# First attention: mixing weights multiplied into the queries, the two decay scales summed before one head sum

## The chip, the cores and the metric

The kernel runs on one core of one Trainium2 chip. The time is the device time of one execution in microseconds (us). The engines are TensorE (PE; PEld is its weight load), VectorE (DVE), ScalarE (ACT), GpSimd (POOL) and SyncE (SP), which issues the DMAs.

## What is computed

Four blocks are added to a residual x of 16 sequences, 256 tokens and 128 channels: the first attention (a), a dense eight-expert feed-forward, a second attention (b), and the feed-forward again. Only the first attention changes. It has 32 heads of 4 channels and two decay scales m. The mixing weight mt is a softmax over the two scales.

```python
phi_q = elu(rope(x @ Wq.T)) + 1            # phi_k likewise
def step(carry, xs):                       # over the tokens
    S, K = carry
    pq, pk, vt, bt, mt = xs
    K = K * bt[..., None] + pk[:, :, None, :]
    S = S * bt[..., None, None] + pk[:, :, None, :, None] * vt[:, :, None, None, :]
    num = einsum('bhd,bhmdc->bhmc', pq, S)
    den = einsum('bhd,bhmd->bhm', pq, K) + EPS
    y = sum(num / den[..., None] * mt[..., None], axis=2)
x = x + layernorm_affine(ln(x) + y @ Wout.T + bout)
```

## The kernel before, in words

The 4096 tokens are cut into 8 tiles of 512 (two sequences). A program loop runs over t = -1 to 9 and, inside, over 32 chunks c (8 experts times 4 slices of 128 hidden units). In step (t, c) each engine's stream first issues its share of the feed-forward of tile t - 2 (`ffn_pe`, `ffn_act`, `ffn_dve`, `ffn_pool`) and then what its own `attn(t, c)` puts at that chunk. So tiles 0 and 1 of the attention run without a feed-forward beside them, tiles 2 to 7 run beside the feed-forward of tiles 0 to 5, and the feed-forward of tiles 6 and 7 has no first attention beside it. The streams are in order; the chunk numbers are an order written out by hand, and semaphores hold what depends.

Feed-forward of a chunk: PE makes `gate` (3 matmuls of 512 columns, split in high and low parts, L338 to L340), `up` (3) and `down` of the chunk three back (3). ACT makes the SiLU (L537) and the high part of the hidden tile (L547). DVE multiplies (L577). The low part (L553) is made by DVE for even chunks and by POOL for odd ones, one chunk later. PE's `up` of a chunk waits for DVE's product of the chunk two back, and `down` waits for the low part. While tile 2 runs, ACT (L461) and POOL (L466) also split the weights of the eight experts.

First attention of a tile, `[128 = 4 channels x 32 heads, 512 tokens]` a piece: PE projects k, q (each twice for the rotation), the two decay rates b0, b1, the mixing logits (mx) and four value pieces v0 to v3 (`project`). DVE makes phi (L1511, c = 10), four products KV = phi_k * v (L1524) and ten scans (L1534): for each scale four numerator components (m, 0) to (m, 3) and one denominator (m, 4). The scanned states are multiplied by phi_q: scale 0 on DVE (L1541: one of 512 and two of 1024), scale 1 on POOL (`product`, L743, five of 512). PE sums over channels with 0/1 matrices in float32: `numerator` (L1107, four per scale, 512 columns), `denominators` (L1117, four of 256 columns) and, once DVE has made weights WGT = (1 + tanh) / den (L1609, L1611, L1616), `weights` (L1128, spreads them to the channels). In the trace each float32 matmul shows as two records. ACT copies the spread weights to RS (L927), DVE multiplies them with the two numerators (`weighted`, L1518), POOL adds the scales to Y (L768), and `project_y` (L1135, L1139) projects Y at chunk 0 of the next tile. The DVE line L1550 takes that result; everything of the next norm and of the residual of this tile follows from it.

## Time and profile before

| | us |
|---|---|
| median of 3 runs | 1755.48 |
| lowest, highest | 1751.98, 1756.20 |
| the profiled execution: its own time | 1751.74 |
| its span | 1749.9 |
| busy: PE | 1625.6 (93%) |
| busy: DVE | 1071.4 (61%) |
| busy: ACT | 1014.7 (58%) |
| busy: POOL | 886.4 (51%) |

The span runs from the first to the last instruction; what is said of durations below is from that one profiled execution. PE records overlap, since a matmul is loaded while the one before it drains: the time that one takes is the distance between starts, not its own duration. The first attention lies in the first 670 us; the second attention lies around 790 to 1170 us, and feed-forwards fill the rest.

### The profile page before, as it was taken

The page shows a single profiled execution, that of the slowest core. Times are in us where ns is not written, and L with a number is a line of the kernel's source. Part 1 is how long each engine was busy: PE and PEld are TensorE (multiplying, and loading weights), DVE is VectorE, ACT ScalarE, POOL GpSimd, SP SyncE. Part 2 cuts the span into 40 slices and gives each one's busy share as a digit, 9 for nine tenths or more (in the row PEclk, how much of TensorE's full clock was granted, in tenths as well). Part 3 has the DMA queues.
Part 4 walks back from the last instruction along what each step waited for, and adds up shares of the span by engine and source line. Part 5 has one row for each costly group of instructions (what it writes and reads, how often), then busy time and mean ns, then how long its engine had stood idle before and what let it go on. Part 6 is the DMA issues. An engine that isn't in the chain of part 4 may idle for free. (4 is left out here: it accounts for less than half of the span.)

```text
span 1749.9 us, 24769 instructions
## 1 busy us (share of the span) xinstructions
PE 1625.6 (93%) x7232; PEld 1253.1 (72%) x7232; DVE 1071.4 (61%) x1871; ACT 1014.7 (58%) x1871; POOL 886.4 (51%) x793
## 2 busy tenths in 40 slices
PE   3588999999999999995899999997999999999998
PEld 2356777777777878883566666665888888888887
DVE  5667777777778685452676676652554555554544
ACT  2236474747464646552577787785555555555554
POOL 3668664646464544333477777784333332333332
PEclk9888999999999999995999999998999999999999
DMA  4035444444443435640000000002555556555553
GB/s 122 1 110 197 151 146 143 145 145 145 141 146 135 145 136 189 212 157 0 1 1 2 2 1 0 1 16 81 181 192 204 194 182 207 193 188 195 195 199 133
DMA packets 72548, 215.88 MB, mean 123 GB/s; under 512 B 7387, under 2 KB 20832, under 8 KB 72416
## 3 DMA queue, kind: packets, MB, share of 16 engines
q1 hardware_dynamic: 72416, 214.35, 35.7%
q8 instruction: 55, 0.90, 0.2%
q14 instruction: 77, 0.63, 0.1%
HBM read 199.64 MB, written 14.68 MB: 122 GB/s over the span
## 5 line engine op out<-in xcount | busy, mean ns | idle before, releaser
L553 POOL TENSOR_TENSOR ARENA_R<-ARENA,ARENA_R 128x512 fp32r<-128x512 f32 x256 | 344.3, 1345 | 605.6 <-ACT ARENA_R L547 604.9
L577 DVE TENSOR_TENSOR ARENA<-ARENA,pair 128x512 f32<-128x512 f32 x512 | 349.2, 682 | 453.7 <-PE pair L340 417.2
L537 ACT ACTIVATE ARENA<-bank 128x512 f32<-128x512 f32 x512 | 306.3, 598 | 471.5 <-PE bank L340 470.5
L338 PE MATMUL pair<-ARENA_R 128*128 128x512 f32 x1064 | 416.9, 392 | 18.6 <-POOL ARENA_R L553 8.3
L340 PE MATMUL pair<-ARENA_R 128*128 128x512 f32 x1064 | 415.0, 390 | 0.0
L339 PE MATMUL pair<-ARENA_R 128*128 128x512 f32 x1064 | 414.3, 389 | 0.0
L547 ACT ACTIVATE ARENA_R<-ARENA 128x512 fp32r<-128x512 f32 x512 | 319.6, 624 | 32.8 <-DVE ARENA L577 30.9
L871 POOL TENSOR_TENSOR ARENA_R<-ARENA,ARENA_R 128x512 fp32r<-128x512 f32 x192 | 249.4, 1314 | 79.9 <-ACT ARENA L1048 76.3
L338 PE MATMUL bank<-ARENA_R 128*128 128x512 f32 x568 | 239.7, 422 | 23.3 <-DVE ARENA L1524 18.1
L338 PEld LDWEIGHTS pair<-ARENA_R 128*128 128x128 f32 x1064 | 200.8, 189 | 67.9 <-POOL ARENA_R L553 10.0
L340 PEld LDWEIGHTS pair<-ARENA_R 128*128 128x128 f32 x1064 | 200.9, 189 | 42.3
L339 PEld LDWEIGHTS pair<-ARENA_R 128*128 128x128 f32 x1064 | 201.1, 189 | 41.2
L339 PE MATMUL bank<-ARENA_R 128*128 128x512 f32 x568 | 223.5, 393 | 0.0
L340 PE MATMUL bank<-ARENA_R 128*128 128x512 f32 x568 | 223.4, 393 | 0.0
L553 DVE TENSOR_TENSOR ARENA_R<-ARENA,ARENA_R 128x512 fp32r<-128x512 f32 x256 | 195.0, 762 | 0.1
L1648 DVE TENSOR_REDUCE ARENA<-bank 128x2 f32<-128x512 f32 (+1 forms) x192 | 131.0, 689 | 86.5 <-PE bank L1257 56.4
L338 PEld LDWEIGHTS bank<-ARENA_R 128*128 128x128 f32 x568 | 108.2, 190 | 52.4 <-DVE ARENA L1524 21.8
L1293 PE MATMUL pair<-ARENA_R 128*128 128x512 f32 x384 | 135.2, 433 | 8.5 <-ACT ARENA L1028 6.9
L1048 ACT ACTIVATE ARENA_R<-pair 128x512 fp32r<-128x512 f32 x192 | 115.6, 602 | 34.4 <-PE pair L1281 26.0
L339 PEld LDWEIGHTS bank<-ARENA_R 128*128 128x128 f32 x568 | 108.4, 191 | 23.5 <-issue 4.3
L340 PEld LDWEIGHTS bank<-ARENA_R 128*128 128x128 f32 x568 | 107.9, 190 | 23.3
L1534 DVE TENSOR_TENSOR_SCAN ARENA<-ARENA 128x512 f32<-128x512 f32 x80 | 121.5, 1526 | 0.0
(213 smaller groups left out, 2037.7 us busy)
## 6 DMA issues: line engine op xcount, KB each, us to landing
ARENA_R<-split_weights SPq DMA_DIRECT2D x360, 512.0 KB, 4.8
split_weights<-ARENA_R SPq DMA_DIRECT2D x24, 512.0 KB, 3.8
X<-in_L_attn_a_x_dram SPq DMA_DIRECT2D x8, 256.0 KB, 5.5
ARENA<-in_L_ffn_Wg_dram SPq DMA_DIRECT2D x8, 256.0 KB, 2.9
ARENA<-in_L_ffn_Wu_dram SPq DMA_DIRECT2D x8, 256.0 KB, 3.2
ARENA<-in_L_ffn_Wd_dram SPq DMA_DIRECT2D x8, 256.0 KB, 3.8
out_dram<-X SPq DMA_DIRECT2D x8, 256.0 KB, 4.3
CST<-in_tables_dram SPq DMA_DIRECT2D x1, 835.5 KB, 4.5
```

The source lines that it names most:

```text
L338: pe.matmul(dst, wh, xh, start=start, stop=False)
L339: pe.matmul(dst, wh, xl, start=False, stop=False)
L340: return pe.matmul(dst, wl, xh, start=False, stop=stop)
L537: act.activation(SG[:, c % 2, :], bank[c % 2], ACT.Silu).then_inc(F.sil, 1)
L547: act.activation(HH[:, G % FC, :], HF[:, G % FC, :], ACT.Copy).then_inc(F.hh, 1)
L553: eng.tensor_tensor(HL[:, G % FC, :], HF[:, G % FC, :], HH[:, G % FC, :].bitcast(F32), ALU.subtract).then_inc(lo_done(G)[0], 1)
L577: v.tensor_tensor(HF[:, c % FC, :], SG[:, c % 2, :], bank[2 + c % 2], ALU.mult).then_inc(F.mul, 1)
L871: g.tensor_tensor(PL[:, u % RING, :], PT[:, u % RING, :], PH[:, u % RING, :].bitcast(F32), ALU.subtract).then_inc(B.pl, 1)
L1048: act.activation(dst[:, u % RING, :], bank[2 + u % 2], ACT.Exp, scale=DB ** -0.5).then_inc(B.t_used, 1)
L1293: m = pe.matmul(bank[4 + qb], VS[:, p, 2 * ob + kb, at:at + P], (PH, PL)[i][:, u % RING, :], start=(u < 2 and i == 0), stop=(g == NG - 1 a ...
L1534: v.tensor_tensor_scan(S[:, m, c, :], BETA[:, m, :], KV[:, c, :], 0.0, ALU.mult, ALU.add).then_inc(A.scan, 1)
L1648: v.tensor_reduce(dst, src, AX.X, ALU.max, negate=True).then_inc(B.row_used, 1)
```

## The change

`PQM[m]` = phi_q times the spread weight of scale m is made on DVE (`weighted`, two of 512, reading PSUM directly). The numerator states are then multiplied by PQM instead of phi_q, scale 0 on DVE (`product`, two of 1024) and scale 1 on POOL (four of 512). POOL adds the two scales component by component (`sum_scales`, four of 512), PE makes one head sum of four float32 matmuls in place of two, and ACT copies it to Y. The two denominator products are both POOL's (`product_z`). ACT's two copies to RS, DVE's 512 product and POOL's addition to Y are gone. The order of the scans, the denominators, the weights and the head sum over the chunks changes with it; `SCANS` lists the new order of the scans for the waits.

```diff
+SCANS = [(0, 4), (1, 4), (0, 0), (0, 1), (1, 0), (0, 2), (0, 3), (1, 1), (1, 2), (1, 3)]
...
+        def scanned(t, m, c):
+            return A.scan, 10 * t + SCANS.index((m, c)) + 1
...
@@ gpsimd
-            def product(t, i):
-                c = (4, 0, 1, 2, 3)[i]
-                g.wait_ge(A.scan, 10 * t + 5 + i + 1)
-                g.wait_ge(A.phi_q, t + 1)
-                g.tensor_tensor(S[:, 1, c, :], S[:, 1, c, :], PQ[:, :], ALU.mult).then_inc(A.prod1, 1)
+            def product_z(t, m):
+                g.wait_ge(*scanned(t, m, 4))
+                g.wait_ge(A.phi_q, t + 1)
+                g.tensor_tensor(S[:, m, 4, :], S[:, m, 4, :], PQ[:, :], ALU.mult).then_inc(A.prodz, 1)
+            def product(t, c):
+                g.wait_ge(*scanned(t, 1, c))
+                g.wait_ge(A.pq, 2 * t + 2)
+                g.tensor_tensor(S[:, 1, c, :], S[:, 1, c, :], PQM[:, 1, :], ALU.mult).then_inc(A.prod1, 1)
+            def sum_scales(t, c):
+                g.wait_ge(A.prod0, 2 * t + c // 2 + 1)
+                g.wait_ge(A.prod1, 4 * t + c + 1)
+                g.tensor_tensor(S[:, 0, c, :], S[:, 0, c, :], S[:, 1, c, :], ALU.add).then_inc(A.sum, 1)
...
-                    if c in (19, 21, 22, 23, 24):
-                        product(t, (19, 21, 22, 23, 24).index(c))
-                    if c == 30:
-                        g.wait_ge(A.ay, 2 * (t + 1))
-                        after(g, A.z, t)
-                        g.tensor_tensor(Y[:, :], RS[:, 0, :], RS[:, 1, :], ALU.add).then_inc(A.y, 1)
+                    if c in (13, 14):
+                        product_z(t, c - 13)
+                    if c in (20, 24, 26, 27):
+                        product(t, (20, 24, 26, 27).index(c))
+                    if c in (23, 25, 27, 28):
+                        sum_scales(t, (23, 25, 27, 28).index(c))
...
@@ scalar
-                    if c == 27:
-                        weight_rows(t, 0)
-                    if c == 28:
-                        weight_rows(t, 1)
+                    if c == CH - 1:
+                        act.wait_ge(A.num, t + 1)
+                        after(act, A.z, t)
+                        act.activation(Y[:, :], bank[7], ACT.Copy).then_inc(A.y, 1)
...
@@ tensor
+                if is_tile(t) and c == 15:
+                    pe.wait_ge(a_used["v2"], t + 1)
+                    denominators(t)
...
-                    if c == 20:
-                        pe.wait_ge(a_used["v3"], t + 1)
-                        numerator(t, 0, (0, 1))
-                    if c == 22:
-                        numerator(t, 0, (2, 3))
-                        pe.wait_ge(a_used["v2"], t + 1)
-                        denominators(t)
-                    if c == 24:
-                        pe.wait_ge(n_a.lo, min(t + 2, NT))
-                        after(pe, n_f.lo, t)
-                        numerator(t, 1, (0, 1))
-                    if c == 25:
-                        numerator(t, 1, (2, 3))
-                    if c == 26:
+                    if c == 18:
                         weights(t, 0)
+                        weights(t, 1)
                     if c == 27:
-                        weights(t, 1)
+                        pe.wait_ge(A.pq, 2 * (t + 1))
+                        numerator(t, (0, 1))
+                    if c == 30:
+                        numerator(t, (2, 3))
...
@@ vector
+                v.wait_ge(A.rep, 2 * t + m + 1)
+                v.wait_ge(A.phi_q, t + 1)
...
+                v.tensor_tensor(PQM[:, m, :], PQ[:, :], bank[(5, 7)[m]], ALU.mult).then_inc(A.pq, 1)
```

DVE's `attn(t, c)` now reads, chunk by chunk: 11 KV 0, scan (0,4); 12 scan (1,4); 13 KV 1 and 2; 14 scan (0,0); 15 KV 3; 16 denominator plus epsilon and reciprocal; 17 WGT, scan (0,1); 18 scan (1,0); 19 `weighted` 0 and 1; 20 scan (0,2); 21 scan (0,3); 22 `product` of components 0 and 1; 23 scan (1,1); 24 `product` of 2 and 3; 25 scan (1,2); 26 scan (1,3). Before, the last scan stood at 23, the reciprocal at 24, WGT at 25 and `weighted` at 28 and 29. Below, L numbers of rows of the kernel before are its own; the changed kernel's are a few lines further on.

DVE in tile 0, from the first KV product, before (L1524 KV, L1534 scan, L1541 product):

```order
L1524 TENSOR_TENSOR ARENA<-ARENA,bank 128x512 x2
L1534 SCALAR_TENSOR_TENSOR ARENA<-ARENA 128x512
L1524 TENSOR_TENSOR ARENA<-ARENA,pair 128x512
L1534 SCALAR_TENSOR_TENSOR ARENA<-ARENA 128x512
L1524 TENSOR_TENSOR ARENA<-ARENA,bank 128x512
L1534 SCALAR_TENSOR_TENSOR ARENA<-ARENA 128x512 x3
L1541 TENSOR_TENSOR ARENA<-ARENA 128x512
L1541 TENSOR_TENSOR ARENA<-ARENA 128x1024
L1534 SCALAR_TENSOR_TENSOR ARENA<-ARENA 128x512
L1541 TENSOR_TENSOR ARENA<-ARENA 128x1024
```

And changed (L1528 KV, L1538 scan, L1594 and L1596 the reciprocal, L1601 WGT, L1522 `weighted`):

```order
L1528 TENSOR_TENSOR ARENA<-ARENA,bank 128x512
L1538 SCALAR_TENSOR_TENSOR ARENA<-ARENA 128x512 x2
L1528 TENSOR_TENSOR ARENA<-ARENA,bank 128x512
L1528 TENSOR_TENSOR ARENA<-ARENA,pair 128x512
L1538 SCALAR_TENSOR_TENSOR ARENA<-ARENA 128x512
L1528 TENSOR_TENSOR ARENA<-ARENA,bank 128x512
L1594 TENSOR_SCALAR ARENA<-pair 128x256
L1596 RECIPROCAL ARENA<-ARENA 128x256
L1601 SCALAR_TENSOR_TENSOR ARENA<-ARENA 128x256
L1538 SCALAR_TENSOR_TENSOR ARENA<-ARENA 128x512 x2
L1522 TENSOR_TENSOR ARENA<-ARENA,pair 128x512
L1522 TENSOR_TENSOR ARENA<-ARENA,bank 128x512
```

The reciprocal has moved from behind all ten scans to behind three of them.

POOL in tile 0, from the first norm's small operations to the end of the tile, before (L743 product, L768 the sum to Y):

```order
L363 TENSOR_SCALAR VE<-MV 128x4
L364 TENSOR_SCALAR NM<-MV 128x4
L366 TENSOR_TENSOR RSTD<-VE,HALF 128x4
L368 TENSOR_TENSOR NB<-NM,RSTD 128x4
L743 TENSOR_TENSOR ARENA<-ARENA 128x512 x5
L768 TENSOR_TENSOR ARENA<-ARENA 128x512
```

And changed (L747 `product_z`, L753 `product`, L759 `sum_scales`):

```order
L371 TENSOR_TENSOR RSTD<-VE,HALF 128x4
L373 TENSOR_TENSOR NB<-NM,RSTD 128x4
L747 TENSOR_TENSOR ARENA<-ARENA 128x512 x2
L753 TENSOR_TENSOR ARENA<-ARENA 128x512
L759 TENSOR_TENSOR ARENA<-ARENA 128x512
L753 TENSOR_TENSOR ARENA<-ARENA 128x512
L759 TENSOR_TENSOR ARENA<-ARENA 128x512
L753 TENSOR_TENSOR ARENA<-ARENA 128x512 x2
L759 TENSOR_TENSOR ARENA<-ARENA 128x512 x2
```

Six large operations have become ten.

## Rows read from the trace of the kernel before

**Rows 1.** The span in 40 equal slices, busy tenths.

```profile
PE   3588999999999999995899999997999999999998
DVE  5667777777778685452676676652554555554544
```

**Rows 2.** Busy time by stretch: tile 0, tile 1, tile 2, tile 4.

```profile
core 0: us, PE busy (x) PEld busy (x) DVE busy (x) ACT busy (x) POOL busy (x), PEclk, DMA share, GB/s
32.10:61.80 29.70, 14.74 (x40) 7.22 (x40) 24.67 (x25) 3.90 (x8) 13.40 (x8) 0.83 0.00 1
78.70:109.10 30.40, 17.12 (x43) 8.57 (x43) 25.38 (x28) 7.55 (x16) 17.40 (x15) 0.72 0.00 1
112.00:212.00 100.00, 91.15 (x364) 69.35 (x363) 75.07 (x103) 58.25 (x109) 80.82 (x63) 0.94 0.53 184
...
420.60:464.40 43.80, 42.07 (x174) 31.49 (x173) 43.54 (x50) 22.35 (x43) 24.12 (x21) 1.00 0.42 142
```

**Rows 3.** Order of time, PE, tile 4 (start, us, line, count), two numerator matmuls.

```profile
443.67 0.39 PE L340 MATMUL pair<-ARENA_R 128*128 128x512 f32 x1
443.90 1.88 PE L1107 MATMUL bank<-ARENA,CST 128*128 128x512 f32 x4
...
445.84 0.40 PE L339 MATMUL bank<-ARENA_R 128*128 128x512 f32 x1
```

**Rows 4.** Order of time, PE, where projection of Y begins, tiles 4 and 5.

```profile
390.72 0.39 PE L1135 MATMUL bank<-BBA,ONESR 128*128 128x512 f32 x1
...
477.48 0.39 PE L338 MATMUL bank<-ARENA_R 128*128 128x512 f32 x1
...
479.52 0.39 PE L1135 MATMUL bank<-BBA,ONESR 128*128 128x512 f32 x1
```

**Rows 5.** Order of time, DVE, tile 4, chunks 10 to 26.

```profile
420.64 0.65 DVE L577 TENSOR_TENSOR ARENA<-ARENA,pair 128x512 f32<-128x512 f32 x1
...
426.15 1.21 DVE L1534 TENSOR_TENSOR_SCAN ARENA<-ARENA 128x512 f32<-128x512 f32 x1
...
449.80 1.40 DVE L553 TENSOR_TENSOR ARENA_R<-ARENA,ARENA_R 128x512 fp32r<-128x512 f32 x1
451.12 2.28 DVE L1534 TENSOR_TENSOR_SCAN ARENA<-ARENA 128x512 f32<-128x512 f32 x1
...
464.44 0.69 DVE L577 TENSOR_TENSOR ARENA<-ARENA,pair 128x512 f32<-128x512 f32 x1 [0.27 <-PE pair L340]
```

**Rows 6.** Order of time, POOL, tile 4.

```profile
449.37 1.28 POOL L743 TENSOR_TENSOR ARENA<-ARENA 128x512 f32<-128x512 f32 x1 [2.89 <-DVE ARENA L1534]
450.61 1.71 POOL L553 TENSOR_TENSOR ARENA_R<-ARENA,ARENA_R 128x512 fp32r<-128x512 f32 x1
```

**Rows 7.** Order of time, DVE, tile 0.

```profile
32.08 1.29 DVE L1511 SCALAR_TENSOR_TENSOR ARENA<-ARENA 128x512 f32<-128x512 f32 x2 [3.62 <-ACT ARENA L916]
...
49.11 3.79 DVE L1534 TENSOR_TENSOR_SCAN ARENA<-ARENA 128x512 f32<-128x512 f32 x2
...
53.24 1.75 DVE L1611 RECIPROCAL ARENA<-ARENA 128x256 f32<-128x256 f32 x1
```

**Rows 8.** Order of time, POOL, tiles 0 and 1.

```profile
44.29 10.89 POOL L743 TENSOR_TENSOR ARENA<-ARENA 128x512 f32<-128x512 f32 x5 [10.86 <-DVE ARENA L1534]
...
84.90 0.80 POOL L368 TENSOR_TENSOR NB<-NM,RSTD 128x4 f32<-128x4 f32 x1
```

**Rows 9.** Order of time, PE, tiles 0 and 1.

```profile
48.23 1.89 PE L1117 MATMUL pair<-ARENA,CST 128*128 128x256 f32 x8
...
61.79 0.51 PE L1135 MATMUL bank<-BBA,ONESR 128*128 128x512 f32 x1 [2.75 <-POOL ARENA L768]
...
109.14 0.77 PE L338 MATMUL bank<-ARENA_R 128*128 128x512 f32 x1 [2.65 <-POOL ARENA_R L466]
```

**Rows 10.** Order of time, DVE, tiles 1 and 2.

```profile
78.69 1.26 DVE L1511 SCALAR_TENSOR_TENSOR ARENA<-ARENA 128x512 f32<-128x512 f32 x2
...
145.01 2.90 DVE L1511 SCALAR_TENSOR_TENSOR ARENA<-ARENA 128x512 f32<-128x512 f32 x2
```

More of the change, by code:

```diff
@@ L252, in program @@
         WGT = take(SEQ)
-        RS = take(MA, TOK)
+        PQM = take(MA, TOK)
         Y = take(TOK)
@@ L922, in half_tanh @@
                                scale=0.5).then_inc(a_used[f"b{m}"], 1)
-            def weight_rows(t, m):
-                act.wait_ge(A.rep, 2 * t + m + 1)
-                after(act, A.y, t)
-                act.activation(RS[:, m, :], bank[5], ACT.Copy).then_inc(A.rs, 1)
             def attn(t, c):
@@ L1125, in weights @@
                 else:
[L1126 removed]
+                    pe.wait_ge(a_used["v3"], t + 1)
                 for b in range(SPT):
[L1128 removed]
+                    x = pe.matmul(bank[(5, 7)[m]][:, b * SEQ:(b + 1) * SEQ], cst(f"rep_{2 * b + m}"), WGT[:, :],
                                   start=True, stop=True)
@@ L1529, in scan @@
                     v.wait_ge(a_used[f"v{c}"], t + 1)
-                    after(v, (A.num0, A.num1)[m], t)
+                    after(v, A.num, t)
                 else:
@@ L1602, in attn @@
                     if c == 22:
+                        product(t, 0, 2)
+                    if c == 23:
+                        scan(t, 1, 1)
+                    if c == 24:
+                        product(t, 2, 4)
+                    if c == 25:
                         scan(t, 1, 2)
-                    if c == 23:
+                    if c == 26:
                         scan(t, 1, 3)
-                    if c == 24:
-                        v.wait_ge(A.den, t + 1)
-                        after(v, A.wgt, t)
-                        v.tensor_scalar(RC[:, :], bank[5][:, 0:SEQ], DEN_EPS, None, ALU.add).then_inc(A.dp, 1)
-                        v.wait_ge(A.dp, t + 1)
-                        v.reciprocal(RC[:, :], RC[:, :]).then_inc(A.rc, 1)
-                    if c == 25:
-                        v.wait_ge(A.rc, t + 1)
-                        v.wait_ge(a_used["mx"], t + 1)
-                        after(v, A.rep, 2 * t)
-                        v.scalar_tensor_tensor(WGT[:, :], MIX[:, :], 1.0, RC[:, :], ALU.add,
-                                               ALU.mult).then_inc(A.wgt, 1)
-                    if c == 28:
-                        weighted(t, 0)
-                    if c == 29:
-                        weighted(t, 1)
             for t in range(-1, NT + 2):
```

73 lines of the change are left out of this document (39 added, 34 removed).

## The prediction, made before the changed kernel ran

> **What bounds the kernel now.** I read the busy tenths first [rows 1]: PE stands at 9 from the fifth slice on, but for two short dips, and at 3 to 8 in the first four (to 175 us); DVE stands at 7 or 8 from the fourth to the thirteenth slice, and at 5 or less in the last third. So I took the busy time by stretch [rows 2]. Three kinds of stretch come out. Tiles 0 and 1 (no feed-forward beside them): PE is busy 14.7 of 29.7 us and DVE 24.7, with gaps; a chain of waits, not an engine, sets the time. Tile 2: PE 91, DVE 75 and POOL 81 of 100 us, since POOL also splits weights. Tile 4, which stands for tiles 3 to 7: over chunks 10 to 25 (43.8 us) PE is busy 42.1 us and DVE 43.5. Both are full there; elsewhere in the tile DVE is not. After tile 7 the change touches nothing.
>
> Next the order of time in those stretches. In tile 4 DVE runs without a gap from 420.64 us (product of chunk 10) and first waits for PE again at 464.44, chunk 26 [rows 5]. So in those chunks PE does not wait for DVE only because its own head sums give DVE time: they lie in chunks 20 to 26.
>
> Two DVE figures recur. A scan alone takes 1.21 us, 1.14 from start to start, and a low part 0.68 (0.60). Beside POOL they take 2.28 and 1.40 [rows 5]: POOL's L743 runs from 449.37 and its L553 from 450.61 to 452.32 [rows 6], and the DVE operations with two operands in SBUF end about one operation after POOL's does. In tile 0 it works both ways: five POOL products that take 1.28 each alone fill 10.89 us [rows 8]. The products that read PSUM keep their 0.65 to 0.69. I therefore count DVE's two-SBUF-operand work and POOL's large operations as taking turns.
>
> The Trainium skill (SBUF — State Buffer, Who interferes with whom) has it that a DVE instruction with two SBUF inputs and a GpSimd instruction that reads SBUF exclude each other for a whole instruction; by that rule the trace agrees on single pairs. On average a POOL operation has cost DVE less than a whole one here, as worked out below.
>
> **The change, part by part.** Eight tiles change.
>
> PE. The group of two float32 matmuls starts at 443.90 and the regular pace (0.227 between starts) resumes at 445.84 [rows 3], so it takes 445.84 - 0.227 - 443.90 = 1.71 us, 0.85 each. Four fewer: -3.4 us a tile. Denominators and weights stay, at other places.
>
> ACT: one copy instead of two, -0.6 us, off the path. DVE: minus a 512 product, 0.6 us. POOL: ten large operations instead of six, +5.2 us a tile.
>
> *Tiles 3 to 7.* DVE from chunk 10 through 26, start to start and without POOL: 17 products 10.0, 8 low parts 4.8, two phi 1.2, four KV 2.4, ten scans 11.4, two 1024 products 2.4, two subtractions 1.2, epsilon and reciprocal 2.1, WGT 0.5, and now both `weighted` too, 1.2: 37.2 us. The same list for the kernel before, through chunk 25, is 36.1, and took 43.8 [rows 5]: 7.7 too much, 0.75 of it in the phi, 6.9 through 13 large POOL operations (eight low parts, five products), 0.53 each. Now there are 15 in the stretch (two `product_z` come in at chunks 13 and 14): 8.0. Then one new wait. `denominators` stands at PE's chunk 15 and needs `product_z` 1, which in POOL's queue lies behind the norm's small operations and a low part. By my walk it ends at 434.1, while PE arrives at 432.5: PE stalls about 1.7 us, and DVE, whose chunk 16 multiplies `up` of that chunk, idles 1.4. Sum 37.2 + 0.75 + 8.0 + 1.4 = 47.4, so the last scan ends at 420.6 + 47.4 = 468.0.
>
> Behind it POOL still has to do `product` 3, `sum_scales` 2, the low part of 27 and `sum_scales` 3: with one clash 5.6 us, to 473.6. PE's chunk 30 waits for it: last head-sum matmul and latency to 474.8, then chunk 31 (9 matmuls, 2.04) to 476.9. In the kernel before, chunk 31 ends at 477.48, two us ahead of the projection at 479.52 [rows 4]. That is -0.6 us a tile instead of -3.4. The period is 479.52 - 390.72 = 88.80 us before [rows 4]; I expect 88.2. The ends: PE hidden by nothing, -3.4; every extra POOL operation at its full 1.3 instead of 0.53, +1.5. Five tiles: **-3 us** (-17 to +7).
>
> *Tile 0.* Before, phi starts at 32.08 [rows 7] and the projection at 61.79 [rows 9]. I walk the new order from 32.08. KV 0 ends at 33.9, scan (0,4) at 35.0, scan (1,4) at 36.2. `product_z` 0 then has its turn to 37.4, scan (0,0) to 38.5, `product_z` 1 to 39.7. PE has had nothing since its transposes, and the granted clock averages 0.83 in this stretch [rows 2]; four 256-column float32 matmuls took 1.89 warm [rows 9], I take 3.0: 42.8. DVE, with nothing left since 39.1, waits 3.7 us. Epsilon and reciprocal (53.24, 1.75) [rows 7]: 45.1. WGT 45.5, two scans 47.8, two `weighted` 49.0. From there DVE's scans and products and POOL's products and sums take turns nearly one to one, as they did from 44.29 on before [rows 8]: `product` 0 of POOL 51.3, scan (0,3) 52.4, subtraction and 1024 product 54.1, scan 55.3, sum 56.4, 1024 product 57.5, POOL product 58.7, scan 59.8, sum 61.0, scan 62.1, and then POOL alone with product 2, product 3, sum 2, sum 3: 67.2. Head sum 68.4, copy 69.1, projection 69.2. Against 61.79: **+7 us** (+4 to +10). The tail behind the last scan is shorter than before (the last scan ended at 52.9 [rows 7], 8.9 us before the projection; now 7.1), but the last scan comes ten us later: reciprocal, WGT and `weighted` now stand ahead of it, 3.8, the denominator wait is 3.7, and the clashes are about 3.
>
> *Tile 1.* From phi at 78.69 [rows 10] to the first feed-forward matmul at 109.14 [rows 9] was 30.45 us. The walk is the same, 35.1 from phi to the last sum, plus about 2 because POOL's two sets of small norm operations run until 85.7 [rows 8], seven us after phi, and `product_z` stands behind them; then one weight part on POOL, 1.3: 38.4. **+8 us** (+4 to +11).
>
> *Tile 2.* POOL is busy 81 of 100 us [rows 2], DVE's chunk 10 begins its phi at 145.01 with 2.90 instead of 1.29 for the pair [rows 10]. DVE and POOL saturate each other, `product_z` waits behind weight parts (I find 4 us at PE's chunk 15), and 4 large operations come in, 5.2 us, while PE's 3.4 us are no gain where PE waits. Nearest rows: +5.2 if all of it lies on the path, 0 if PE's saving pays it. **+5 us** (0 to +9).
>
> Sum: 7 + 8 + 5 - 3 = +17 us. The profiled execution took 1751.74, so 1768.7; it lies 3.7 under the median of the three runs, and on the median 1755.48 the sum is **1772.5 us**.
>
> **The rivals.** (1) *PE's saving survives.* If DVE's chunks drain faster than I count (fewer clashes, no wait at chunk 15), tiles 2 to 7 get 3.4 each, -20; with the lower ends of tiles 0 and 1, +8, and 0 to +6 for what PE's stall in tile 2 leaves, the total is -12 to -6: about 1748. For it: PE is busy 42.1 of 43.8 us, so every us taken from it is room. Against it: DVE is busy 43.5 of the same. It decides if DVE can finish chunk 26 before about 465.5. This is the case on the other side of no change.
>
> (2) *A wash.* The prologue costs its lower ends, +8, tile 2 +2 and the steady tiles -1.5 each: +2.5, 1758. For it: a walk always lets two things collide that miss each other on the chip.
>
> (3) *The port, not the queue, decides.* If each added POOL operation holds DVE for its whole length, tiles 3 to 7 cost +1.5 instead of -0.6: +10 more, 1783. For it: single pairs behave so [rows 5, 6]. Against it: the average of 0.53 in the same stretch. This is what the exclusive lock that the Trainium skill states (SBUF — State Buffer, summary table) would make of it if the added operations always came first.
>
> (4) *The change does not do what it says*: PE keeps all its matmuls, or the order is the old one. The orders above exclude it; no chance.
>
> **How the numbers follow.** Forecast (+10 to +24 us) 0.58; rival 3 0.14; rival 2 0.16; rival 1 0.12. 0.3% is 5.3 us, about what a measurement of this kernel can tell from no change. Faster by more: most of rival 1, 0.10. Within: rival 2 and a little of the first, 0.17. Slower: 0.73. The range leaves out most of rival 1 below and the last of rival 3 above: 1756 to 1786.
>
> **What would show it.** PE has 64 fewer float32 records of the head sum (64 instead of 128, 0.85 us a matmul). Projection of tile 0 at about 69 us instead of 61.8, with a DVE gap of 2 to 4 us ahead of the epsilon line, and ten us more from phi to the last scan. In tile 1, about 38 us from phi to the first feed-forward matmul. Period of tiles 3 to 7 near 88.2 us, with PE gaps ahead of the denominators (released by POOL's `product_z`) and of the second half of the head sum (released by `sum_scales`), which were none before, and DVE without a gap from chunk 17 to 26. I would be wrong if the period fell to 86 us or less (PE's saving survives), or if the first projection came before 64 us.

## The result, and the profile after

| | kernel before | changed kernel |
|---|---|---|
| median (lowest to highest) | 1754.64 us (1751.98 to 1756.2), 4 runs | 1772.96 us (1772.31 to 1773.14), 4 runs |
| own time of the profiled execution | 1751.74 us | 1772.87 us |
| its span, mean granted clock | 1749.9 us, 0.969 | 1771.1 us, 0.960 |

The changed kernel takes 1.0105 times the time of the one before, 95% interval 1.0088 to 1.0123: slower by 18.3 us between medians. The forecast was 1772.5. The profiled execution of before lies 3 us under its median, that of the changed kernel on its own; between the two profiled executions, and so in everything read from traces below, the difference is 21 us.

To place it, I use milestones that both traces have: the start of the phi operations in tiles 0 and 1, and DVE's first read of the output projection in each tile (the reader, a few us behind the matmul that the prediction calls the projection of Y).

| us | before | changed | difference | forecast |
|---|---|---|---|---|
| start of phi, tile 0 | 32.08 | 32.61 | +0.5 | 0 |
| phi to reader, tile 0 | 31.14 | 39.66 | +8.5 | +7 |
| reader to phi of tile 1 | 15.47 | 16.38 | +0.9 | 0 |
| phi to reader, tile 1 | 39.03 | 45.58 | +6.6 | +8 |
| reader to reader, tile 1 to 2 | 100.00 | 105.18 | +5.2 | +5 |
| four periods to tile 6, each | 88.80 | 88.85 | +0.2 in all | -0.6 each |
| period to tile 7 | 88.13 | 87.69 | -0.4 | -0.6 |
| reader of tile 7 | 661.04 | 682.51 | +21.5 | +17 |

Behind the last reader both kernels take 1089 us. The loss lies before the reader of tile 2, which comes after 218 us in the kernel before and after 239 us in the changed one.

The page of the changed kernel shows it in its slices. The first line is busy time (share of the span) and instructions by engine, then come busy tenths of the span in 40 slices of 44.3 us, and the granted clock in tenths:

```profile
PE 1612.2 (91%) x7168; PEld 1240.4 (70%) x7168; DVE 1083.5 (61%) x1863; ACT 1010.0 (57%) x1863; POOL 937.6 (53%) x825
...
PE   4458799999999999996799999997999999999998
...
DVE  4567859696969596453566666762555554554544
...
PEclk9659999999999999997799999998999999999999
```

PE stood at 8, 8 and 9 in the third to fifth slices before [rows 1]; now it reads 5, 8 and 7. The granted clock is at 6 and 5 tenths in the second and third slices. The busy time by stretch, for tile 0 (phi to projection), tile 1 (phi to the first feed-forward matmul) and tile 4 (product of chunk 10 to the last scan), answers to [rows 2]:

```profile
core 0: us, PE busy (x) PEld busy (x) DVE busy (x) ACT busy (x) POOL busy (x), PEclk, DMA share, GB/s
32.60:69.70 37.10, 16.06 (x31) 7.76 (x31) 26.75 (x24) 3.34 (x7) 18.76 (x12) 0.60 0.00 0
88.60:127.00 38.40, 17.11 (x36) 9.08 (x36) 26.46 (x28) 5.96 (x13) 23.95 (x20) 0.54 0.00 0
442.40:490.20 47.80, 43.98 (x190) 34.21 (x189) 46.34 (x53) 24.31 (x46) 29.38 (x24) 1.00 0.46 163
```

In tile 0 PE has 31 records where it had 40, but is busy 16.1 us instead of 14.7: each takes longer. The granted clock fell from 0.83 to 0.60 in tile 0 and from 0.72 to 0.54 in tile 1. In tile 4 it is 1.00, as before.

**Tile 0 in order of time** (start, duration, what is written from what, and in brackets the idle time before it and its releaser). DVE, which answers to [rows 7]:

```profile
32.61 1.29 DVE L1513 SCALAR_TENSOR_TENSOR ARENA<-ARENA 128x512 f32<-128x512 f32 x2 [3.63 <-ACT ARENA L932]
...
42.98 0.42 DVE L1594 TENSOR_SCALAR ARENA<-pair 128x256 f32<-128x256 f32 x1 [2.27 <-PE pair L1127]
...
48.43 0.69 DVE L1522 TENSOR_TENSOR ARENA<-ARENA,bank 128x512 f32<-128x512 f32 x1
...
57.30 4.42 DVE L1538 TENSOR_TENSOR_SCAN ARENA<-ARENA 128x512 f32<-128x512 f32 x2
```

POOL, with both `product_z` (L747), the last two products (L753) and the last two sums over the scales (L759):

```profile
35.72 3.32 POOL L747 TENSOR_TENSOR ARENA<-ARENA 128x512 f32<-128x512 f32 x2 [1.75 <-DVE ARENA L1538]
...
60.59 3.39 POOL L753 TENSOR_TENSOR ARENA<-ARENA 128x512 f32<-128x512 f32 x2
63.95 2.48 POOL L759 TENSOR_TENSOR ARENA<-ARENA 128x512 f32<-128x512 f32 x2
```

PE, with the denominators, the second half of the head sum and the projection; the first and last answer to [rows 9]:

```profile
39.18 3.75 PE L1127 MATMUL pair<-ARENA,CST 128*128 128x256 f32 x8 [3.66 <-POOL ARENA L747]
...
65.26 3.78 PE L1118 MATMUL bank<-ARENA,CST 128*128 128x512 f32 x4 [2.50 <-POOL ARENA L759]
69.73 0.79 PE L1145 MATMUL bank<-BBA,ONESR 128*128 128x512 f32 x1 [0.69 <-ACT ARENA L960]
```

The chain can be followed through the three: `product_z` ends at 39.04, the denominators at 42.93, the epsilon line follows with 2.27 us of idle DVE ahead of it, the last scan ends at 61.72, the last sum at 66.43, the head sum at 69.04. Two of these steps have doubled: the denominators took 1.89 us in the kernel before [rows 9] and take 3.75, and the four records of two head-sum matmuls took 1.88 at the full clock [rows 3] and take 3.78.

Tile 1 is the same with more of it: phi at 88.65, 4.94 us of idle DVE, the first feed-forward matmul at 126.94, 38.3 us after phi (38.4 was forecast; 30.45 before).

```profile
101.44 0.42 DVE L1594 TENSOR_SCALAR ARENA<-pair 128x256 f32<-128x256 f32 x1 [4.94 <-PE pair L1127]
```

```profile
126.94 1.42 PE L339 MATMUL bank<-ARENA_R 128*128 128x512 f32 x1
```

**Tile 4, PE**, from one projection to the next. The period by these two rows is 501.38 - 412.53 = 88.85 us, against 88.80 [rows 4]; between them the denominators, both halves of the head sum and every row at which PE waited by more than 0.3 us:

```profile
412.53 0.39 PE L1145 MATMUL bank<-BBA,ONESR 128*128 128x512 f32 x1
...
446.89 0.50 PE L339 MATMUL bank<-ARENA_R 128*128 128x512 f32 x1 [1.26 <-DVE ARENA L1528]
...
453.03 0.66 PE L432 MATMUL bank<-CST,ARENA 128*128 128x128 f32 x4 [1.04 <-DVE ARENA L1528]
...
455.59 1.89 PE L1127 MATMUL pair<-ARENA,CST 128*128 128x256 f32 x8
...
482.05 0.50 PE L339 MATMUL pair<-ARENA_R 128*128 128x512 f32 x1 [1.16 <-DVE ARENA L582]
...
486.47 1.88 PE L1118 MATMUL bank<-ARENA,CST 128*128 128x512 f32 x4
...
492.21 0.50 PE L339 MATMUL pair<-ARENA_R 128*128 128x512 f32 x1 [0.39 <-DVE ARENA_R L558]
...
495.42 2.01 PE L1118 MATMUL bank<-ARENA,CST 128*128 128x512 f32 x4
...
501.38 0.39 PE L1145 MATMUL bank<-BBA,ONESR 128*128 128x512 f32 x1
```

The same rows of the kernel before, over its period:

```profile
425.09 0.50 PE L338 MATMUL bank<-ARENA_R 128*128 128x512 f32 x1 [1.27 <-DVE ARENA L1524]
...
442.44 0.47 PE L338 MATMUL pair<-ARENA_R 128*128 128x512 f32 x1 [0.47 <-DVE ARENA L577]
...
468.33 1.13 PE L1128 MATMUL pair<-ARENA,CST 128*128 128x256 f32 x4 [0.30 <-ACT ARENA L927]
```

I took the time from start to start of PE's matmuls over the regular 0.2275 us, where no group of another kind explains it: 1.43, 0.63 and 0.47 in the kernel before, 2.5 us in all; 1.42, 1.20, 1.32, 0.29, 0.40, 0.56, 0.24, and 0.14 inside the last head-sum group now, 5.6 us. The difference, 3.1 us, is close to the 3.4 us of matmul time that the change saved. The PE time went into PE's own waits for DVE, and the period stayed. One of them comes from the new order of DVE's stream: `f_turn` (L432) reuses the bank of `v1`, which KV 1 reads, and KV 1 has moved from chunk 11 to 13.

### The profile page after: what moved, and what is told of

It reads as the page before. It is cut to its first block and busy times, and to the rows that moved or that the text cites. A ratio compares the mean times of both kernels' runs of the same rounds, so it can differ in the third digit from the quotient of the medians.

```text
span 1771.1 us, 24674 instructions
## 1 busy us (share of the span) xinstructions
PE 1612.2 (91%) x7168; PEld 1240.4 (70%) x7168; DVE 1083.5 (61%) x1863; ACT 1010.0 (57%) x1863; POOL 937.6 (53%) x825
## 5 line engine op out<-in xcount | busy, mean ns | idle before, releaser
L558 DVE TENSOR_TENSOR ARENA_R<-ARENA,ARENA_R 128x512 fp32r<-128x512 f32 x256 | 204.4, 798 | 0.6
L1538 DVE TENSOR_TENSOR_SCAN ARENA<-ARENA 128x512 f32<-128x512 f32 x80 | 138.7, 1742 | 0.0
L1059 ACT ACTIVATE ARENA_R<-pair 128x512 fp32r<-128x512 f32 x192 | 115.6, 602 | 33.8 <-PE pair L1283 25.9
```

The costliest lines, as they stand in the source:

```text
L558: eng.tensor_tensor(HL[:, G % FC, :], HF[:, G % FC, :], HH[:, G % FC, :].bitcast(F32), ALU.subtract).then_inc(lo_done(G)[0], 1)
L1059: act.activation(dst[:, u % RING, :], bank[2 + u % 2], ACT.Exp, scale=DB ** -0.5).then_inc(B.t_used, 1)
L1538: v.tensor_tensor_scan(S[:, m, c, :], BETA[:, m, :], KV[:, c, :], 0.0, ALU.mult, ALU.add).then_inc(A.scan, 1)
```

## The experiments

Most kernels ran once, with a profile. Their single time is good to a few us, since executions of the kernel before spread over 4.2 us; so I read them by the milestones. The changed kernel, the first experiment and the one with the later `v3` have the same PE work up to the reader in tiles 0 and 1, and give 39.66, 39.57, 39.62 us and 45.58, 45.57, 45.55: a tenth is what such a figure is good for there, and 0.05 us for the periods. The kernel before with the later `v3` (e13) has as many matmuls in tile 0 as the kernel before, and its projection met the lower clock, which cost 1.1 us. So 1.1 us in tile 0 of a kernel traced once may be no more than when the clock fell.

| kernel | time | tile 0, phi to reader | tile 1 | to tile 2 | four periods, each | last | reader of tile 7 |
|---|---|---|---|---|---|---|---|
| before | 1754.64 | 31.14 | 39.03 | 100.00 | 88.80 | 88.13 | 661.04 |
| changed | 1772.96 | 39.66 | 45.58 | 105.18 | 88.85 | 87.69 | 682.51 |
| e1_scans_early | 1773.07 | 39.57 | 45.57 | 105.15 | 88.86 | 87.76 | 682.6 |
| e5_no_scale_sum | 1743.35 | 34.08 | 40.08 | 101.60 | 86.32 | 85.13 | 654.2 |
| e2_tensor_adds_scales | 1757.91 | 33.96 | 40.33 | 102.18 | 88.78 | 87.72 | 666.6 |
| e3_before_half_head_sum | 1754.79 | 34.37 | 41.36 | 99.94 | 88.47 | 87.76 | 665.4 |
| e9_filler_matmuls | 1765.34 | 35.40 | 43.17 | 105.14 | 88.86 | 87.68 | 675.0 |
| e11_before_filler | 1752.17 | 31.14 | 37.56 | 100.87 | 88.81 | 88.12 | 660.7 |
| e8_scans_in_both_gaps | 1752.77 | 31.01 | 37.83 | 101.50 | 88.78 | 87.77 | 661.1 |
| e10_both_gaps_and_filler | 1750.99 | 31.16 | 35.44 | 102.39 | 88.79 | 87.74 | 659.5 |
| e14_after_v3_later | 1773.39 | 39.62 | 45.55 | 105.28 | 88.65 | 88.14 | 682.0 |
| e13_before_v3_later | 1758.16 | 32.24 | 38.46 | 101.56 | 89.14 | 88.45 | 666.1 |
| e12_all_v3_later | 1749.35 (11 runs) | 30.48 | 36.35 | 102.72 | 88.53 | 88.24 | 660.0 |

### Does the DVE gap ahead of the reciprocal cost tile 0 its time?

Two scans that the gap has room for are moved ahead of the epsilon line, in tiles 0 and 1 alone.

```diff
+                    if c == 16 and t < 2:
+                        scan(t, 0, 1)
+                        scan(t, 1, 0)
                     if c == 16:
                         v.wait_ge(A.den, t + 1)
...
-                        scan(t, 0, 1)
-                    if c == 18:
+                    if c == 17 and not t < 2:
+                        scan(t, 0, 1)
+                    if c == 18 and not t < 2:
                         scan(t, 1, 0)
```

> The changed kernel with one edit: in tiles 0 and 1 alone, scans (0,1) and (1,0) stand ahead of the epsilon line and the reciprocal instead of behind WGT, where DVE waits 2.3 and 4.9 us for the denominators. Theory (the loss in tiles 0 and 1 is a chain on DVE, and the wait for the denominators is a part of it): phi to the first projection (tile 0) falls from 37.1 to about 35, phi to the projection's reader in tile 1 from 45.6 to about 43.3, the whole by about 4.5 us against the changed kernel, to 1768. Rival (the loss there is TensorE's, by stalls and a lower granted clock): no more than 1 us, since TensorE has the same gaps.

Measured: 39.57 and 45.57 us, nothing gained, where the theory had two us in each tile. DVE's rows from the epsilon line on, of this kernel:

```profile
43.13 0.42 DVE L1597 TENSOR_SCALAR ARENA<-pair 128x256 f32<-128x256 f32 x1
...
47.03 0.69 DVE L1522 TENSOR_TENSOR ARENA<-ARENA,pair 128x512 f32<-128x512 f32 x1 [1.22 <-PE pair L1138]
48.50 0.69 DVE L1522 TENSOR_TENSOR ARENA<-ARENA,bank 128x512 f32<-128x512 f32 x1 [0.78 <-PE bank L1138]
```

The 2.27 us ahead of the epsilon line are gone, and 1.22 + 0.78 us stand ahead of the two `weighted`. The second `weighted` starts at 48.50, in the changed kernel at 48.43. So the gap was not itself the price. The path runs through `product_z`, denominators, reciprocal, WGT, the matmuls of the weights and `weighted`; the scans fill it from either side, and moved from one gap they open the other. Whether filling both gaps at once pays is tried further down.

### What do POOL's sums over the scales cost?

The sums are left out; PE reads scale 0 alone once both products are there.

```diff
-                    if c in (23, 25, 27, 28):
-                        sum_scales(t, (23, 25, 27, 28).index(c))
...
-                    pe.wait_ge(A.sum, 4 * t + c + 1)
+                    pe.wait_ge(A.prod0, 2 * t + c // 2 + 1)
+                    pe.wait_ge(A.prod1, 4 * t + c + 1)
```

> The changed kernel without sum_scales (four 512-column additions on POOL a tile); the head sum reads scale 0 alone, so the sum over the scales is left out. TensorE's work is the same. Theory (POOL's additions hold DVE's scans back and are the tail of the chain): tiles 0 and 1 about -4.6 us each, tile 2 -3 to -5, tiles 3 to 7 -1 to -2 each, 1748 to 1755 in all. Rival (the steady tiles are held by DVE's own work, the additions hide there): tiles 3 to 7 unchanged at 88.85, 1760 or more.

Measured: 5.6 us in tile 0, 5.5 in tile 1, 3.6 in tile 2 and 2.5 in each later tile, 28 us to the reader of tile 7. The full tiles gain more than the 1 to 2 us expected. Of its four operations of 1.3 us, each costs 0.63 in a full tile. In tile 0 not all of the 5.6 us is theirs: up to the projection's first matmul it is 4.5 (65.20 - 32.55 against 69.73 - 32.61), 1.1 an operation, and the other 1.1 lies behind it, where PE's eight projection records take 1.05 us instead of 1.91, since the granted clock over 60 to 80 us is 0.84 here and 0.65 in the changed kernel. That the later tiles gain is what bears most on the theory: without the sums the rest of the change (four matmuls fewer on PE, one product fewer on DVE) makes the period 88.80 - 86.32 = 2.5 us shorter than before. PE's saving was real, and POOL's sums took it back.

The price in a full tile is close to the average of 0.53 us that the prediction read from the kernel before; that in tile 0 is near a whole operation. The Trainium skill (SBUF — State Buffer, Who interferes with whom) has the port pair as an exclusive lock; where the two engines run little else, as in tile 0, the trace agrees (0.65 us of a product that reads PSUM is untouched, a scan of 1.21 grows to 2.27 beside `product_z`); in a full tile the added operations cost half of what it would make of them. Why half is not shown: each of the sixteen sums of tiles 3 to 6 runs beside a product that reads PSUM and keeps its length, and also beside a low part that is stretched.

### Would PE add the scales more cheaply?

PE adds both scales into one bank, with eight matmuls as in the kernel before. Everything else of the change stays: weights into the queries, `product_z`, denominators early.

```diff
-                    pe.wait_ge(A.sum, 4 * t + c + 1)
-                    x = pe.matmul(bank[7], cst(f"sum_{c}"), S[:, 0, c, :], start=(c == 0), stop=(c == DA - 1))
+                    pe.wait_ge(A.prod0, 2 * t + c // 2 + 1)
+                    pe.matmul(bank[7], cst(f"sum_{c}"), S[:, 0, c, :], start=(c == 0), stop=False)
+                    pe.wait_ge(A.prod1, 4 * t + c + 1)
+                    x = pe.matmul(bank[7], cst(f"sum_{c}"), S[:, 1, c, :], start=False, stop=(c == DA - 1))
...
-                    if c == 27:
+                    if c == 24:
                         pe.wait_ge(A.pq, 2 * (t + 1))
-                        numerator(t, (0, 1))
-                    if c == 30:
-                        numerator(t, (2, 3))
+                    if c in (24, 26, 28, 30):
+                        numerator(t, (c // 2 - 12,))
```

> The changed kernel with the scales added on TensorE: no sum_scales, eight float32 matmuls into one bank, one component of both scales at chunks 24, 26, 28 and 30. TensorE has as many head-sum matmuls as before the change, POOL as many large operations. Theory: tiles 0 and 1 about -4 us each, tile 2 -3 to -5, tiles 3 to 7 between -1 and +1 each (the four matmuls come back, into time in which TensorE waits for DVE, and the tail on POOL is gone), about 1761 in all. Rival (TensorE's work sets tiles 3 to 7): +2 to +3.4 in each of them, 1772 to 1778.

Measured: 1757.91 us, 15 less than the changed kernel. The periods are 88.78, as before and as changed, so in full tiles the edit trades 3.4 us of PE for the 2.5 of POOL and neither shows. Against the kernel without sums (86.32), which differs by these four matmuls and their chunks, the matmuls cost 2.5 us a tile: that is what they are worth once POOL's sums are gone. Nearly the whole gain lies in tiles 0 to 2: -5.7, -5.3 and -3.0. In tile 0 it is as quick as the kernel with no sum at all (33.96 and 34.08): there four more matmuls on PE cost nothing on balance (the granted clock over 60 to 80 us is 0.91, and 0.84 without them). What still separates it from before, +2.8 in tile 0 and +1.3 in tile 1, is the chain through the denominators.

### Is PE's clock part of the loss?

The clock rows above say that less work on PE in a stretch of waits goes with a lower clock. To have that without the change: the kernel before, with half of its head-sum matmuls.

```diff
-                    x = pe.matmul(bank[(7, 6)[m]], cst(f"sum_{c}"), S[:, m, c, :], start=(c == 0), stop=(c == DA - 1))
+                    if c % 2:
+                        x = pe.matmul(bank[(7, 6)[m]], cst(f"sum_{c}"), S[:, m, c, :], start=(c == 1), stop=(c == DA - 1))
```

> The kernel before with the head sum of components 1 and 3 alone: four of its eight float32 matmuls a tile are left out (the others' products and waits stay), nothing else. This is the change's saving on TensorE by itself. Theory (DVE is as full as TensorE over chunks 10 to 25): less than half of the 3.4 us a tile shows, the period of tiles 3 to 7 falls from 88.8 to 87.5 to 88.5, 1745 to 1752 in all. Rival (TensorE bounds those tiles and the change's new order loses the gain): the period falls by 3 or more to 85.5, 1735 or less.

Measured: tile 0 is 3.2 us longer, tile 1 2.3, the periods 0.33 shorter, and the time 1754.79, that of the kernel before with less to compute. The period is in the expected range, the time is not (1745 to 1752): a loss in tiles 0 and 1 had not been thought of. Busy time in two stretches of this kernel and then of before:

```profile
32.00:60.00 28.00, 13.75 (x29) 6.59 (x30) 23.99 (x24) 3.36 (x7) 12.18 (x7) 0.68 0.00 0
...
80.00:108.00 28.00, 13.18 (x28) 6.30 (x29) 25.15 (x32) 4.40 (x10) 18.37 (x14) 0.62 0.00 0
```

```profile
32.00:60.00 28.00, 14.73 (x39) 7.21 (x39) 24.30 (x25) 4.00 (x9) 12.24 (x7) 0.82 0.00 1
...
80.00:108.00 28.00, 17.12 (x43) 8.57 (x43) 24.08 (x24) 6.46 (x14) 15.24 (x13) 0.74 0.00 1
```

In the first stretch the granted clock is 0.68 instead of 0.82, in the second 0.62 instead of 0.74. The matmuls that are left sit on the path, and they are the ones that now take twice as long:

```profile
59.03 2.08 PE L1129 MATMUL pair<-ARENA,CST 128*128 128x256 f32 x4 [0.69 <-ACT ARENA L927]
...
63.86 0.80 PE L1136 MATMUL bank<-BBA,ONESR 128*128 128x512 f32 x1 [2.75 <-POOL ARENA L768]
```

The row of the kernel before that answers to the first:

```profile
57.91 1.13 PE L1128 MATMUL pair<-ARENA,CST 128*128 128x256 f32 x4 [0.69 <-ACT ARENA L927]
```

The four records of the second weights took 2.08 us instead of 1.13; the projection's first matmul 0.80 instead of 0.51 [rows 9]. Of the 3.2 us, 1.1 lies behind the projection, and that part alone may be no more than when the clock fell (e13, below). The steady part answers a second question: in full tiles PE's 3.4 us are worth only 0.33 in the kernel before. PE now waits where it did not, longest ahead of a head sum:

```profile
466.90 1.10 PE L1108 MATMUL bank<-ARENA,CST 128*128 128x512 f32 x2 [1.99 <-POOL ARENA L743]
```

The releaser is POOL's product, which itself had waited for DVE's scan. So DVE's scans hold POOL, and through it PE.

The other way round: the changed kernel, with filler matmuls into a bank that nothing reads, ahead of and behind its waits, in tiles 0 and 1.

```diff
+            def warm(t, n):
+
+                if 0 <= t < 2:
+                    for _ in range(n):
+                        pe.matmul(bank[0], ONESR[:, :], LAH[:, 0:4, :].rearrange("p a b -> p (a b)"), start=True,
+                                  stop=True)
...
                     if c == 12:
+                        warm(t, 6 if t == 0 else 22)
...
                 if is_tile(t) and c == 15:
+                    warm(t, 8 if t == 0 else 7)
...
+                        warm(t, 3)
                         weights(t, 0)
                         weights(t, 1)
+                        warm(t, 24)
```

(eight more behind each of the first two components of the head sum)

> The changed kernel with filler matmuls (512 columns, float32r, into a bank that nothing reads) on TensorE in tiles 0 and 1, in gaps in which it waited: 6 and 22 ahead of v3, 8 and 7 ahead of the denominators, 3 ahead of the weights, 24 behind them, 8 behind each of the first two head-sum components. No other engine gets work. Theory (half or more of the loss in tiles 0 and 1 is the granted clock, which fell from 0.82 to 0.64 in 32 to 60 us, so that denominators, weights, the end of the head sum and the projection take twice as long on the path): phi to the reader of the projection falls from 39.7 to about 35.5 (tile 0) and from 45.6 to about 43 (tile 1), about -6 us in all, 1767. Rival (the chain of DVE and POOL alone, as forecast): at most -1 us in each tile, or a loss where fillers are late.

Measured: -4.3 us in tile 0, -2.4 in tile 1, -0.45 between the two (reader to phi), nothing in the later tiles; 1765.34 us, 7.6 under the changed kernel. Busy time in tile 0, of this kernel and then of the changed one:

```profile
32.00:60.00 28.00, 18.37 (x75) 13.10 (x74) 26.78 (x24) 2.89 (x7) 14.76 (x9) 1.00 0.00 1
```

```profile
32.00:60.00 28.00, 10.20 (x25) 6.14 (x25) 25.04 (x24) 3.35 (x8) 12.85 (x9) 0.64 0.00 0
```

and its PE rows, to be laid beside those of the changed kernel above:

```profile
38.74 1.97 PE L1136 MATMUL pair<-ARENA,CST 128*128 128x256 f32 x8 [1.81 <-POOL ARENA L747]
...
63.09 2.35 PE L1118 MATMUL bank<-ARENA,CST 128*128 128x512 f32 x4 [1.63 <-POOL ARENA L759]
66.13 0.50 PE L1154 MATMUL bank<-BBA,ONESR 128*128 128x512 f32 x1 [0.69 <-ACT ARENA L960]
```

The granted clock is 1.00, the upper of its two levels (2.4 GHz), throughout; the denominators take 1.97 instead of 3.75 us, the second half of the head sum 2.35 instead of 3.78. Counted from phi, the last sum on POOL ends 1.7 us earlier, the projection starts 3.15 earlier and the reader 4.3. So 4.3 of tile 0's 8.5 us and 2.4 of tile 1's 6.6 can be had back by the clock alone, in matmuls that something waits for. The Trainium skill (TensorE: Matmul & The Clock Gate, What's actually happening) puts it as "the default state is throttled, and activity releases the throttle"; the three clock readings 0.82, 0.64 and 1.00 of this stretch, with 39, 25 and 75 records, agree.

The control is a like filling in the kernel before (6 and 22 matmuls ahead of `v3`, 20 and 6 ahead of the head sum, 8 behind the second weights; in tile 0 that is 34 where the changed kernel had 57).

```diff
+                        warm(t, 6 if t == 0 else 22)
...
                     if c == 20:
+                        warm(t, 20 if t == 0 else 6)
...
                         weights(t, 1)
+                        warm(t, 8)
```

> The kernel before with the same filler matmuls in tiles 0 and 1: 6 and 22 ahead of v3, 20 and 6 ahead of the head sum, 8 behind the weights. Its granted clock was 0.82 and 0.74 there. If the clock is part of the change's loss, less is to be had here than in the changed kernel: -1 to -3 us, 1750 to 1752. Rival (fillers help wherever the chain crosses TensorE, by the same amount): -6.

Measured: 0 in tile 0, -1.5 in tile 1, +0.9 in tile 2; 1752.17 us. The granted clock over 32 to 60 us rose here too, from 0.82 to 0.94. The filler is therefore no gain in itself: it gives back only what a kernel has lost to the clock. For tile 0 the whole 4.3 us is then a loss of the change; of tile 1's 2.4 us, 1.5 could be had in the kernel before as well, so 0.9 is left. In the kernel before, PE's own head sums lie in the waits; with half of them gone, above, the clock fell. Why tile 2 lengthens was not looked into.

### Fill both gaps, and let PE add the scales

```diff
+                    if c == 16 and t < 2:
+                        scan(t, 0, 1)
+                        scan(t, 1, 0)
...
+                    if c == 19 and t < 2:
+                        scan(t, 0, 2)
+                        scan(t, 0, 3)
                     if c == 19:
                         weighted(t, 0)
```

(on top of PE adding the scales; the four scans go from their old places in tiles 0 and 1)

> The kernel whose TensorE adds the scales (1757.9), with, in tiles 0 and 1 alone, scans (0,1) and (1,0) ahead of the reciprocal and (0,2) and (0,3) ahead of weighted, so that DVE has work in both waits of the chain denominators, reciprocal, WGT, weights, weighted. Theory (two waits lie one behind the other on that chain; filling the first alone, as tried, moved the idle time into the second): about -2.5 us a tile, 1753. Rival (the two scans only delay weighted): 0 to +1 a tile.

Measured: 31.01 and 37.83 us, 2.9 and 2.5 less than with PE adding the scales alone, and 1752.77 us. DVE has no idle time left from its phi to its last scan. With both gaps filled the rest of tile 0's loss is gone: 31.01 against 31.14 before. This is the form of the first experiment that works. The filler comes on top of it:

> The kernel of the run before this one with the filler matmuls of the changed kernel's run (16 behind the weights, none between the components). If filling DVE's waits and holding the clock add up: about -4 us more, 1749, below the kernel before. Rival: the fillers are in the way of a chain that now waits less for TensorE, 0 to +2.

Measured: tile 0 31.16, tile 1 35.44 (-2.4), tile 2 102.39 (+0.9), 1750.99 us, 1.8 under the kernel without them where 4 were expected. The fillers (6 and 22 matmuls ahead of `v3`, 8 and 7 ahead of the denominators, 3 and 16 about the weights) are worth nothing in tile 0 here, though the granted clock over 32 to 60 us rises from 0.70 to 0.88 and the denominators take 2.00 us instead of 3.75: with scans in both of DVE's gaps nothing waits for these matmuls, and the projection already ran at the full clock. What tile 1 gains, tile 2 gives back in part.

### PE's two waits in the full tiles

PE waits 1.26 us at `v3` (chunk 12) and 1.04 us at the transposes of `f_turn` (chunk 14), both released by DVE's KV products (L1528). Both steps are put one chunk later.

```diff
-                    if c == 12:
+                    if c == 13:
                         pe.wait_ge(a_used["v0"], t + 1)
...
-                if is_tile(old) and c == 14:
+                if is_tile(old) and c == 15:
                     if is_tile(t):
```

(`f_hi` and `f_lo`, which read the transposes, go from chunk 15 to 16)

> The changed kernel with v3 projected at chunk 13 instead of 12 and the transposes of the feed-forward's norm at 15 instead of 14 (their copy and subtraction at 16), which takes away two waits of TensorE for DVE's KV products, 1.3 and 1.0 us a tile. No engine gets or loses work. Theory (in tiles 3 to 7 the changed kernel is bound by DVE and POOL from chunk 10 to the end of the sums, so what TensorE wins there it waits for later): the period stays within 0.4 us of 88.85, 1771 to 1774. Rival (each stall of TensorE adds to the period): -2 to -2.3 us a tile, 1760.

Measured: -0.2 us a tile (88.65) and +0.45 in tile 7, 0.5 less to the reader of tile 7, and 1773.39 us, no gain in the time. The row that answers to the waits removed:

```profile
454.37 1.97 PE L1127 MATMUL pair<-ARENA,CST 128*128 128x256 f32 x8 [1.01 <-POOL ARENA L747]
```

This is the wait that the prediction had put in the changed kernel, the denominators behind `product_z`. There it was not to be seen (455.59, no idle) because PE had already lost as much a chunk earlier; with that wait gone it appears, 1.01 us.

> The kernel before with v3 at chunk 13 instead of 12, one wait of 1.3 us of TensorE a tile taken away. Leaving out half the head sum gave 0.33 us a tile there, so this gives as little: period 88.5 to 88.8, 1750 to 1755. Rival (TensorE bounds the tile): -1.3 a tile, 1745.

The kernel before with its `v3` one chunk later took 1758.16 us, 6 more than the kernel before beside it: +1.1 in tile 0, +1.6 in tile 2, and 0.34 in each full tile, where a gain or nothing had been the question. The 1.1 us of tile 0 lie behind the projection's first matmul, which came at the lower clock:

```profile
62.50 0.80 PE L1135 MATMUL bank<-BBA,ONESR 128*128 128x512 f32 x1 [2.75 <-POOL ARENA L768]
```

It took 0.51 us in the kernel before [rows 9], and the reader follows it by 2.54 us instead of 1.43. In the full tiles the wait at `v3` is gone, and PE waits 0.96 and 0.94 us for DVE's product (L577) at two chunks, where it waited 0.47 at one; what makes the tile longer than before, and not only as long, is open.

> The kernel whose TensorE adds the scales, with both gaps filled and the filler matmuls (1751.0), and v3 and the transposes one chunk later as above. There POOL's additions are gone and TensorE does not wait for DVE or POOL after chunk 15 in tiles 3 to 7, so the same edit should pay: -1 to -2.2 us a tile, period 86.6 to 87.8, 1740 to 1746, faster than both kernels by 0.4 to 0.8%. If DVE bounds it all the same: 1751.

Everything together (PE adds the scales, scans in both gaps, filler, the later `v3` and `f_turn`) took 1749.35 us (1747.83 to 1752.05, 11 runs) beside 1752.06 us (1750.98 to 1753.98, 15 runs) of the kernel before: ratio 0.9985, interval 0.9976 to 0.9994. It beats both kernels, by 2.7 us over the one before; 1740 to 1746 had been expected. Its row at the denominators says why in part:

```profile
432.51 1.96 PE L1134 MATMUL pair<-ARENA,CST 128*128 128x256 f32 x8 [1.01 <-POOL ARENA L747]
```

This wait, and one of 0.45 us for DVE's product at 427.09, have taken the place of the two removed (1.28 and 1.08), and the period is 88.53 instead of 88.79: 0.26 us. The rest of the difference was not placed.

## Why the prediction was right, and where it was not

**The total.** 1772.5 against 1772.96, with the sign, the place and the order of size of every stretch but one. Part of its closeness is luck. Between the profiled executions the steps add to +21.5, not +17; the profiled execution of before lay low, and setting the sum on the median of before put 3.7 us on top. The two nearly cancel, and within the sum tile 1 to its reader (+6.6 for +8) hides part of what tile 0 and the full tiles cost more.

**Tile 0, +7, measured +7.4 to the projection and +8.5 to the reader.** From phi to the projection's first matmul 37.1 us had been forecast (69.2 - 32.08), and 69.73 - 32.61 = 37.1 came out. The walk held at nearly every point, counted from phi: denominators done after 10.7 us (10.3 measured), second `weighted` done 16.9 (16.5), last scan done 30.0 (29.1), last sum 35.1 (33.8), projection 37.1 (37.1). The 1.3 us by which it was ahead at the last sum went into the head sum and its copy, taken as 2 us and measured as 3.3, at the slower clock. What lies behind, projection to reader and on to phi of tile 1, was taken as unchanged, and is 1.1 and 0.9 us longer: PE's eight projection records took 1.91 us at the lower clock, and 1.05 in tile 4.

**The reasons given for tile 0** were only partly right. The prediction split "ten us" to the last scan into 3.8 for reciprocal, WGT and `weighted`, 3.7 for the denominator wait, and 3 for clashes, as if each could be had back by itself. Its own walk gives 9.2 (62.1 - 52.9) and not ten; measured from phi it is 8.3 (29.1 against 20.8). The first experiment shows that the wait can't: 2.27 us of it filled gave nothing. What could be had back, measured one at a time, is 5.7 by taking the sums from POOL, 4.3 by PE's clock, and with the sums gone 2.9 by filling both gaps; these overlap, since their sum is over 8.5, and 1.1 of the 5.7 is itself the clock, back by the time of the projection. The step that was mis-sized is "I take 3.0" for the denominators: it was 3.75, and the clock was treated as a surcharge on one step, where it fell over the whole stretch, because the change removes PE's work from it.

**Tile 1, +8, measured +7.8** from phi to the first feed-forward matmul, and **tile 2, +5, measured +5.2**. In tile 2 the forecast had put the whole of four POOL operations on the path; without them it is 3.6 us shorter, so they are most of it. The rest was not looked into, so that 5 came out as 5.2 is in part luck.

**Tiles 3 to 7, -3, measured -0.2.** The last scan was due 47.4 us after the product of chunk 10 and ended after 47.8:

```profile
442.44 0.65 DVE L582 TENSOR_TENSOR ARENA<-ARENA,pair 128x512 f32<-128x512 f32 x1
...
488.27 1.95 DVE L1538 TENSOR_TENSOR_SCAN ARENA<-ARENA 128x512 f32<-128x512 f32 x1
```

The last sum was due after 53.0 us and ended after 53.8:

```profile
494.50 1.75 POOL L759 TENSOR_TENSOR ARENA<-ARENA 128x512 f32<-128x512 f32 x1
```

Each is under a us off, but 0.6 was all that had been left of the 3.4, and the last 0.8 is more than that. So the mechanism (POOL's added operations hold DVE back and PE's saving turns into waits) was right and the term mis-sized, by 0.6 us a tile. Its place was wrong: PE doesn't stand at the denominators and hardly at the second half of the head sum, but at `f_turn` (L432), whose wait for the moved KV 1 the walk had left out, and at feed-forward matmuls that DVE releases (1.16 and 0.39 us, the others under 0.25). And DVE is not without a gap in chunks 17 to 26: it waits 0.75 us for PE at 467.23.

**Signs that were named.** There are 64 records of the head sum for 128, 592 ns in the median and 1222 at most. The projection of tile 0 came at 69.73 (about 69), the DVE gap was 2.27 (2 to 4), tile 1 took 38.3 (38). From phi to the last scan it was 8.3 us more, not ten. The period was 88.85 and not 88.2, and PE's gaps were not ahead of the denominators.

**The rivals.** That PE's saving survives would have needed full tiles of 85.4 us. The experiment without the sums came to 86.32, so it named the right condition, which the change doesn't meet. The port held for whole operations would have made the periods 90.3; they are 88.85. (The prediction got +1.5 by adding two operations at 0.77 each, and should have added that to its -0.6, which makes 89.7; that was not met either.) The wash had tiles 0 and 1 at +8 in all; they are at +15.

## What to carry to other kernels

Work taken from a full engine is worth what the next one lets through: here PE's 3.4 us a tile were worth 0.33 in the kernel before, where DVE is full, 2.5 with POOL's sums gone, and nothing as the change stood. In a stretch bound by a chain of waits, list the chain first: a gap in it can be filled only with work off the chain, and moving such work from one gap to the next gains nothing. And look at PE's clock before taking matmuls out of such a stretch, since those that stay may take twice as long.

## What the runs showed of the hardware that was not expected

A kernel with fewer matmuls was slower by it: four of eight head-sum matmuls left out of the kernel before lengthen tile 0 by 3.2 us and tile 1 by 2.3, at a granted clock of 0.68 for 0.82 in the first of them. And matmuls whose result nobody reads made the changed kernel 7.6 us faster. The prediction took 3.0 us for a group that takes 1.89 at the full clock, but not that the matmuls the change removes would move the clock of all that stay.
